# One-core adaLN block with gated linear attention and experts: four rotating PSUM banks with a table instead of two in turn

## The reference

```
h = layernorm(x) * (1 + ca) + sa
x = x + ga * attention(h)
h = layernorm(x) * (1 + cb) + sb
x = x + gb * (experts(h) + sigmoid(h @ sg) * shared(h))
```

```
o     = (Q e^G) @ S + tril(Qh @ Kh^T) @ V
S_new = S * e^glast + Ks^T @ V
out   = (o * rsqrt(mean(o*o) + eps) * norm_w * silu(h @ Wgate)) @ Wo
```

## Time and profile before

| | us |
|---|---|
| three runs | 458.25, 461.17, 461.62; median 461.17 |
| the profiled execution | 459.07 |
| its span | 457.3 |
| TensorE busy, mean granted clock | 401.1 (88%), 0.95 |
| VectorE, ScalarE, GpSimd busy | 238.7, 146.0, 147.7 |

### The profile page before, as it was taken

How to read it: one execution, slowest core, us unless ns; L and a number is a source line. 1 busy time by engine, 2 the same in 40 slices (tenths; PEclk the granted TensorE clock), 3 DMA queues, 4 the chain that set the end, 5 groups by cost and what they waited for, 6 DMA issues and landing times.

```text
span 457.3 us, 9813 instructions
## 1 busy us (share of the span) xinstructions
PE 401.1 (88%) x3848; PEld 245.4 (54%) x3849; DVE 238.7 (52%) x559; ACT 146.0 (32%) x295; POOL 147.7 (32%) x249
## 2 busy tenths in 40 slices
PE   3988889898989998998799999825999999999785
PEld 3434565575547575645544744612466666666353
DVE  3167556698588469221652552002255565565467
ACT  2566627444644422162022311000243333333000
POOL 8304104110510051020000057773017677677400
PEclk9999899998999799799899999975999999999899
DMA  8999000000000000084000012323023333321097
GB/s 262 296 309 240 3 5 1 3 3 4 0 3 4 1 1 4 2 268 114 0 0 0 2 47 106 107 106 106 0 83 105 89 122 97 84 92 47 32 313 238
DMA packets 31230, 37.72 MB, mean 82 GB/s; under 512 B 4176, under 2 KB 28115, under 8 KB 31189
## 3 DMA queue, kind: packets, MB, share of 16 engines
q1 hardware_dynamic: 27780, 28.63, 21.2%
q0 software_dynamic: 3408, 8.51, 5.3%
HBM read 21.15 MB, written 16.90 MB: 83 GB/s over the span
## 4 chain that ended last, share of the span: by engine, by line
PE 70%; DVE 8%; ACT 6%; another core or an unknown queue 6%; issue 4%; DMA 4%; SPq 1%; DVEq 0%; POOLq 0%; ACTq 0%
PE work L1295 13%; PE at_ps L1630 11%; PE work L1325 7%; PE work L1305 4%; PE work L1651 4%; PE work L1499 4%; PE at_ps L1360 3%; PE work L1653 3%; PE work L1445 3%; DMA arena<-ys_tokens 2%; PE at_ps L1348 2%; PE at_ps L1614 2%; PE work L1436 2%; PE o_even L1413 2%
## 5 line engine op out<-in xcount | busy, mean ns | idle before, releaser
L582 POOL DMA_INDIRECT ys_tokens<-er_pos,goal_u x39 | 43.8, 1123 | 44.3 <-DVE er_pos L1218 38.5
L1305 PE MATMUL work<-sdn_sb,hs 128*128 128x256 f32 x192 | 48.5, 396 | 8.9 <-issue 4.7
L1630 PE MATMUL at_ps<-arena 128*128 x156 | 54.5, 472 | 0.4 <-ACT arena L802 0.4
L553 POOL DMA_INDIRECT xs_sorted<-h2tok,pos_u x32 | 31.6, 987 | 72.0 <-DVE pos_u L910 62.6
L984 DVE TENSOR_TENSOR hs<-work,hs 128x512 f32<-128x512 f32 (+1 forms) x24 | 16.6, 692 | 63.8 <-PE work L1295 50.4
L598 ACT ACTIVATE hs<-work 128x512 f32<-128x512 f32 (+1 forms) x24 | 14.3, 596 | 103.1 <-PE work L1295 85.5
L1305 PEld LDWEIGHTS work<-sdn_sb,hs 128*128 128x128 f32 x192 | 34.0, 189 | 22.5 <-issue 12.4
L516 POOL TENSOR_TENSOR sq<-sq,sg 128x512 f32<-128x512 f32 x8 | 10.0, 1276 | 100.1 <-issue 100.1
L1295 PE MATMUL work<-h2T,sup_sb 128*128 128x512 f32 x80 | 37.9, 623 | 0.6 <-DVE hs L984 0.3
L1630 PEld LDWEIGHTS at_ps<-arena 128*128 128x128 f32 x156 | 26.5, 190 | 14.9 <-issue 6.6
L806 ACT ACTIVATE arena<-at_ps 128x176 f32<-128x176 f32 x39 | 12.4, 318 | 59.7 <-PE at_ps L1630 43.6
(11 more groups left out here) (225 smaller groups left out, 776.8 us busy)
## 6 DMA issues: line engine op xcount, KB each, us to landing
xs_sorted<-arena SPq DMA_DIRECT2D x10, 526.0 KB, 10.3
h2tok<-xs_sorted SPq DMA_DIRECT2D x20, 263.0 KB
arena<-ys_tokens SPq DMA_DIRECT2D x8, 512.0 KB, 7.3
arena<-in_e_up SPq DMA_DIRECT2D x8, 352.0 KB, 5.4
x_sb<-in_x SPq DMA_DIRECT2D x4, 512.0 KB, 7.4
out_rows<-x_sb SPq DMA_DIRECT2D x16, 128.0 KB, 4.8
sup_sb<-in_s_up SPq DMA_DIRECT2D x2, 640.0 KB, 4.7
hs<-in_wmod SPq DMA_DIRECT2D x1, 1024.0 KB, 8.2
```

What stands on the lines that cost most here:

```text
L553: g.indirect_dma_start(out=xs_dram, out_offset=bass.IndirectOffsetOnAxis(ap=pos_u[:, k, t:t + 1], axis=0), in_=h2tok[:, t, :], in_offset=N ...
L582: g.indirect_dma_start(out=ys_dram, out_offset=bass.IndirectOffsetOnAxis(ap=goal_u[:, i:i + 1], axis=0), in_=yout[:, q % 2, u, :], in_offs ...
L1305: ins = t_.matmul(o[:, t * HID:(t + 1) * HID], hs[0:m, f, tk], sdn_sb[0:m, f, :], start=(f == 0), stop=(f == FTS - 1))
L1630: ins = t_.matmul(at_ps[2 + u % 2][:, 0:2 * FE], xT[:, u % 2, k * P:(k + 1) * P], eup[:, bass.ds(e, 1), k, :].rearrange("p a n -> p (a n)" ...
```

## The change

The rotating ring gets four banks: `work[0]`, `work[1]`, `at_ps[2]`, `at_ps[3]`. For the products of slots 0 to 3 a fixed table says which bank each uses (`BANKS`); from slot 4 on, banks 0 and 1 are used in turn as before. `begin` waits for the last product in the same bank (`LAST_IN_BANK`), not for the product two places ahead. Z becomes a product of the ring, in banks 2 and 3. KV leaves the ring: its halves go to `at_ps[0]` and `at_ps[1]`, with a semaphore `kv_full` of their own. The modulation rows of the second batch row go to `o_ps`.

Four places in TensorE's order change. K half 0 moves up between HT and RT. The two halves of KV move up: half 0 stands behind WO half 0, half 1 behind LR. G half 1 is taken apart: the first halves of the scores' quarters (q = 0, 1) stand before its first matmul, the other two quarters between its two pairs. The waits for `kh_ready` and `qeo_ready` stand ahead of G half 0. On VectorE `next_state(s)` moves up, between `add_out(b, 0)` and `add_out(b, 1)` (in slot 0 between `finish_mod_rows(0)` and `scale_wo()`), and so ahead of `z_min(s + 1)`.

The core of the diff:

```diff
+BANKS = {("G", 0): 0, ("G", 1): 1, ("V", 0): 0, ("HT", 0): 1, ("HT", 1): 0, ("K", 0): 1, ("RT", 0): 0, ("K", 1): 2,
+         ("Q", 0): 3, ("Q", 1): 1, ("V", 1): 0, ("KT", 0): 2, ("KT", 1): 3, ("XT", 0): 1, ("XT", 1): 0, ("WO", 0): 2,
+         ("LR", 0): 3, ("WO", 1): 1, ("Z", 0): 2, ("Z", 1): 3}
...
+BANK_OF = dict(UNITS)
+LAST_IN_BANK = {key: next((k for k, w in reversed(UNITS[:n]) if w == at), None) for n, (key, at) in enumerate(UNITS)}
...
+                "Z": [(zabs_done, 2 * blk + j + 1), (zmin_done, 2 * blk + j + 1)],
...
         def bank(key):
-            return work[TURN[key] % 2]
+            return (work + at_ps[2:])[BANK_OF[key]]
...
                 if b >= 0:
                     gated_out(b)
-                    add_out(b)
+                    add_out(b, 0)
                 else:
                     finish_mod_rows(0)
+                if s < NBLK:
+                    next_state(s)
+                if b >= 0:
+                    add_out(b, 1)
+                else:
                     scale_wo()
                 if s + 1 < NBLK:
                     z_min(s + 1)
-                if s < NBLK:
-                    next_state(s)
...
             def begin(key):
-                n = TURN[key]
-                if n >= 2:
-                    for s, val in released(UNITS[n - 2]):
+                if LAST_IN_BANK[key]:
+                    for s, val in released(LAST_IN_BANK[key]):
                         pe.wait_ge(s, val)
...
-            def scores_first(b):
+            def scores_first(b, first_q, last_q):
-                for q in range(2 * KC):
+                for q in range(first_q, last_q):
                     for j in range(NPAIR):
+                        if q == 0 and j == 0:
+                            pe.wait_ge(kvin_ready, 2 * b + 2)
                         if q == 0 and j == KC:
-                            pe.wait_ge(zabs_done, 2 * b + 2)
-                            pe.wait_ge(zmin_done, 2 * b + 2)
+                            pe.wait_ge(zabs_done, 2 * min(b + 2, NBLK))
+                            pe.wait_ge(zmin_done, 2 * min(b + 2, NBLK))
...
-            def key_values(s):
-                pe.wait_ge(ktok_ready, 2 * s + 2)
-                pe.wait_ge(v_ready, 2 * s + 2)
...
+            def key_values(s, e):
+                if e == 0:
+                    pe.wait_ge(ktok_ready, 2 * s + 2)
+                    pe.wait_ge(v_ready, 2 * s + 2)
+                    if s == 0:
+                        pe.wait_ge(modr_ready, 2)
+                    else:
+                        pe.wait_ge(mln_done, 2 * s)
...
                     project(("G", s, 0), wgate_sb, 0, hT)
...
+                    if b >= 0:
+                        scores_first(b, 0, KC)
+                        project(("G", s, 1), wgate_sb, 1, hT, between=lambda: scores_first(b, KC, 2 * KC))
                     else:
-                        pe.wait_ge(modr_ready, 2 * BATCH)
-                    scores_first(b)
-                if s < NBLK:
-                    project(("G", s, 1), wgate_sb, 1, hT)
+                        project(("G", s, 1), wgate_sb, 1, hT)
...
+                    project(("K", s, 0), wk_sb, 0, hT)
+                if h >= 0:
...
                     router(h)
...
+                if s < NBLK:
+                    key_values(s, 0)
                 if s + 1 < NBLK:
                     low_rank(s + 1)
+                if s < NBLK:
+                    key_values(s, 1)
...
                 if s + 1 < NBLK:
                     gate_logits(s + 1)
-                if s < NBLK:
-                    key_values(s)
```

More of the change, by code:

```diff
@@ L55 @@
 SH_F = [(f * P, min(P, FS - f * P)) for f in range(FTS)]
+BANKS = {("G", 0): 0, ("G", 1): 1, ("V", 0): 0, ("HT", 0): 1, ("HT", 1): 0, ("K", 0): 1, ("RT", 0): 0, ("K", 1): 2,
+         ("Q", 0): 3, ("Q", 1): 1, ("V", 1): 0, ("KT", 0): 2, ("KT", 1): 3, ("XT", 0): 1, ("XT", 1): 0, ("WO", 0): 2,
+         ("LR", 0): 3, ("WO", 1): 1, ("Z", 0): 2, ("Z", 1): 3}
 def unit_order():
-    units = [("MODC", 0, 0)]
-    def both(kind, blk):
-        units.extend([(kind, blk, 0), (kind, blk, 1)])
-    def fill(s, place):
-        for part, blk, i in FILL.get((s, place), ()):
-            units.extend([("SD", blk, i)] if part == "D" else [("SA", blk, i)] + [("SB", blk, i)][:i < FTS - 1])
@@ L68, in unit_order, with put, turn, part @@
-    both("XT", 0)
-    units.append(("LR", 0, 0))
-    for s in range(NBLK + 1):
-        b, h = s - 1, s - 2
-        if s < NBLK:
-            both("G", s)
-        fill(s, "gates")
-        if s < NBLK:
-            units.append(("V", s, 0))
+    units = [(("MODC", 0, 0), 0)]
+    def put(kind, blk, j):
+        units.append(((kind, blk, j), BANKS[kind, j]))
+    def turn(*keys):
+        for key in keys:
+            units.append((key, 1 - units[-1][1] % 2))
+    def part(kind, blk, i):
+        turn(*([("SD", blk, i)] if kind == "D" else [("SA", blk, i)] + [("SB", blk, i)][:i < FTS - 1]))
@@ L77, in unit_order @@
+    def fill(s, place):
+        for kind, blk, i in FILL.get((s, place), ()):
+            part(kind, blk, i)
+    for kind, j in (("XT", 0), ("XT", 1), ("LR", 0), ("Z", 0), ("Z", 1)):
+        put(kind, 0, j)
+    for s in range(NBLK):
+        b, h = s - 1, s - 2
+        put("G", s, 0)
+        put("G", s, 1)
+        put("V", s, 0)
         if h >= 0:
-            both("HT", h)
+            put("HT", h, 0)
+            put("HT", h, 1)
+        put("K", s, 0)
         if h >= 0:
-            units.append(("RT", h, 0))
@@ L81, in unit_order @@
-        fill(s, "half")
-        fill(s, "second")
-        if s < NBLK:
-            both("K", s)
-        fill(s, "norm")
-        if s < NBLK:
-            both("Q", s)
-            units.append(("V", s, 1))
-            both("KT", s)
+            put("RT", h, 0)
+        for kind, j in (("K", 1), ("Q", 0), ("Q", 1), ("V", 1), ("KT", 0), ("KT", 1)):
+            put(kind, s, j)
         if s + 1 < NBLK:
-            both("XT", s + 1)
+            put("XT", s + 1, 0)
+            put("XT", s + 1, 1)
@@ L100, in unit_order @@
+    fill(NBLK, "half")
+    fill(NBLK, "second")
+    fill(NBLK, "norm")
+    turn(("WO", NBLK - 1, 0), ("WO", NBLK - 1, 1))
     fill(NBLK, "stats")
     fill(NBLK, "ln")
-    both("HT", NBLK - 1)
+    turn(("HT", NBLK - 1, 0), ("HT", NBLK - 1, 1))
     fill(NBLK, "transposed")
-    units.append(("RT", NBLK - 1, 0))
+    turn(("RT", NBLK - 1, 0))
     fill(NBLK, "top2")
@@ L107, in unit_order @@
     for f in range(EARLY_UP, FTS):
-        units.extend([("SA", NBLK - 1, f)] + [("SB", NBLK - 1, f)][:f < FTS - 1])
-    both("SD", NBLK - 1)
+        part("U", NBLK - 1, f)
+    turn(("SD", NBLK - 1, 0), ("SD", NBLK - 1, 1))
     return units
```

114 lines of the change are left out of this document (54 added, 60 removed).

## The result

| | before | changed |
|---|---|---|
| median of the runs, us | 461.08 (4 runs, 458.25 to 461.62) | 449.06 (4 runs, 445.96 to 450.14) |
| profiled execution, its span | 459.07, 457.3 | 445.96, 444.2 |
| granted clock, mean | 0.950 | 0.966 |
| first indirect DMA of the scatter, us | 267.14 | 254.97 |

The ratio is 0.9738 (95% interval 0.9684 to 0.9791). All ratios here leave out executions over 1.5% slower than the fastest one of the same kernel; the medians take all. The medians differ by 12.0 us, where 9.0 were forecast. The forecast was 452.1; the rival "the clock comes back everywhere" had 447.4. What was measured lies between them, nearer to the rival.

A forecast was written before the change was run, and what follows sets the result against it. Slots 0 to 3 were taken as bound by TensorE's own work plus short waits on a two-bank ring. 8.4 - 0.6 - 0.2 - 0.15 - 0.3 + 1.9, say 9.0, off 459.07, plus 2.1, gave 452.1 us; range 447.0 to 457.5.

The forecast's parts named there:

- the clock comes back everywhere: Rival: all 6.6 us lost to low clock in slots 1 to 3 return, not 1.9; 447.4 us, chance 0.20.
- G behind KV: Start of slots 1 to 3: G's waits for VectorE's read-out of KV all go, 3.4 us.
- KT; V half 1 of slot 0: KT's four waits for V's read-out go, 1.9 us; V half 1's wait for Q in slot 0 goes, 1.3.
- router of slots 2 and 3: K half 0 between HT and RT covers the two waits for HT's read-out, 1.5 us gained.
- WO: WO's waits for XT go, 0.3 us; in slot 3 WO half 0 comes 0.15 before KT half 0 is read.
- scores' wait for Z, and taking apart: First scores wait for Z's read-out, 0.2 us three times, 0.6 lost; cutting G half 1 and KV costs 0.3.
- XT in slot 2: XT waits for ScalarE's rows if K's read-out ends late; 0.2 us lost, bounds 0 and 1.0.
- holes for "issue": TensorE's holes called "issue", 5.2 us in this stretch, stay or land elsewhere: 0, bounds plus and minus 1.7 us.
- clock, slots 1 to 3: Of 6.6 us lost to low clock, 1.5 from the first fall and 0.4 of the rest return, 1.9.
- the waits change place: Rival: scores wait for Z, XT for its rows, the clock returns nothing; gain 4.0, 457.2 us, chance 0.15.
- Slower: Rival: openings of slots 1 to 3 lose 32-row overlap and the clock falls; 7 us slower, 468, chance 0.05.
- Swallowed later: Rival: longer "issue" holes or clock falls in slot 4 take the gain; 461 us, chance 0.08.

The follow-up runs named there:

- r3: Changed kernel with KV whole behind Z again and the next state behind Z's read-out on VectorE; 426.44 us, ratio 0.9687.
- r4: Changed kernel with all four moves of the order undone, only the four banks and their table kept; 430.28 us, ratio 0.9762.
- r2: Changed kernel with K half 0 put back behind the second share of the chunks; 433.33 us, ratio 0.9826.
- r5: Changed kernel with the scores whole ahead of G half 1 again; 432.78 us, ratio 0.9770.
- r6: Changed kernel with VectorE reading Z out ahead of the second addition to x; 433.98 us, ratio 0.9815.
- r8: Changed kernel with KV whole behind Z and the next state behind Z's read-out in slots 0 to 2, both early only in slot 3; 427.86 us, ratio 0.9696.
- r10: Changed kernel with the ten DMAs that zero the rows held until both halves of slot 0's KV are made; 442.76 us (one run).
- r9: r8 with the scores whole ahead of G half 1 as well; 428.00 us, ratio 0.9700.
- r12: The kernel of r3 once more, in more rounds; 430.37 us, ratio 0.9653.
- r7: Changed kernel with the router of slots 2 and 3 held by four more ScalarE copies of HT half 1; 439.67 us, ratio 0.9946.
- r11: The changed kernel once more, with no edit, as a further sample of its clock; 430.51 us, ratio 0.9777.
- r1: The changed kernel again, with no edit, on another chip as its yardstick; 430.32 us, ratio 0.9749.

## Why the prediction was right, point by point

| step | taken, us | measured, us |
|---|---|---|
| G behind KV | +3.4 | +3.4, but by the banks alone (r3, r4) |
| KT; V half 1 of slot 0 | +1.9; +1.3 | gone, both |
| router of slots 2 and 3 | +1.5 | gone; r2 brings back 1.6 |
| WO | +0.3 - 0.15 | -0.2 (0.3 before, 0.5 after) |
| scores' wait for Z, and taking apart | -0.6 - 0.3 | -3.7 |
| XT in slot 2 | -0.2 (to -1.0) | -1.2 |
| holes for "issue", the scores' apart | 0 | -0.2: KV's 0.6 became 2.0, the others fell from 2.7 to 1.5 |
| HT | not named | -0.3 (0.4 before, 0.7 after) |
| clock, slots 1 to 3 | +1.9 (to +6.6) | +6.6, 5.1 of it by K half 0 (r2, r4) |

By the measured sizes: 8.4 (with all of WO's 0.3) - 0.5 - 3.7 - 1.2 - 0.2 - 0.3 + 6.6 = 9.1. Another 0.5 is an earlier start of slot 0 (19.5 for 20.0). Slot 4 came 11.4 earlier; 1.8 of that has no row of its own.

Direction and mechanism of the waits were right: every wait that was to go went, at the forecast size, and the two that were to stay stayed. The sum was right partly by luck. The clock gave 4.7 more than taken, and the other rows 4.65 less (scores and taking apart 2.8, XT 1.0, WO 0.35, HT 0.3, "issue" 0.2): they cancel to a tenth. And by two of the prediction's own signs it was wrong: "The forecast is wrong if XT or the scores wait a microsecond or more", and XT waited 1.2 us and the scores 1.0 in slot 2; and the first scores were to take not clearly over 1.2 us in sum, where in slot 2 their three pieces take 1.94.

*"Of the other 5.0 I take 0.4, since small products still stand together there."* That is the term that was furthest off. The small products do still stand together; the clock stays up. The router of slots 2 and 3 (from 101 and 141 us in the changed kernel) was followed by full clock in every kernel with K half 0 ahead of the router and the router not held (the changed one three times, r3, r5, r6, r8 and r10, also r9 and r12, whose fall at 115 us lies behind XT) and by a fall in both slots in every kernel with a hole there (before, r2, r4, r7), 0.7 to 3.5 us behind the router's start. Slot 4's router keeps its wait of 0.7 us in every kernel, and there the clock fell 0.5 to 2.8 us behind its start in ten of the fourteen profiles (in the changed kernel at 175 us, behind 173.3) and was already low in three; in r3 it stayed up. The rival "the clock comes back everywhere" had this right and got 0.20. The rule quoted beside it, short idle times between groups that cycle through PSUM banks make the clock swing ("TensorE: Matmul & The Clock Gate" in the Trainium skill), is borne out here in its first part, with holes of 0.8 us. The cycling through banks is not what counts at the router: it waits for ScalarE's copy of HT, and in r4, with the waits for banks gone, both falls stayed.

*"Price 0 to 0.5 each; I take 0.2"* and *"I take 0.3, near the abutting rows."* Together 3.7. The first counted VectorE's instructions right and missed that GpSimd's product, moved to the same time, blocks one of them. It took the addition to x as ending at T + 0.9; it ended at T + 1.8, of which 0.74 is the block and 0.3 a scan that ended later than taken. The second was judged by rows in which G is followed by the scores once. A single split of the scores costs 0.3 to 0.4 us (r3, r4, r5), about what was taken in sum for all. The state early accounts for 2.1 of the 3.7: r3 gets them back.

*XT* lost 1.2 instead of 0.2. From the end of K's read-out to the end of ScalarE's rows there are 7.0 us (108.42 to 115.46), as computed, and TensorE needs 7.9 from K's end (106.4) to XT, for the 8.2 computed. But K's read-out ended 2.0 us behind K, where before it was 0.9 (113.1, 114.0) and the wait begins at 1.2. VectorE did not lose time, TensorE won it: from the start of slot 2 to K's end it needed 24.2 us before (88.9 to 113.1) and 23.4 now, since the router's waits and the low clock are gone. Waits that go and a clock that rises bring the next reader's deadline forward; the terms weren't independent. r2, r4 and r7, which have the router's holes and falls, don't wait at XT.

The rival "the waits change place" (0.15) was thus half true, 3.7 + 1.2 lost where it had 3.4 + 1.0; the clock, to which it gave nothing, made the difference. "Slower" asked for two falls and none came. "Swallowed later" neither: 11.4 at slot 4, 12.2 at the scatter, 13.1 in the span.

What stays open is slot 1. The clock fell between 40 and 75 us in r5, r6, r7, r9 and r10, in none of the three profiles of the changed kernel, nor in r2, r3, r4, r8 and r12. The falls before 50 us (r5, r6, r7) stand in or right behind KV's hole, in three of the seven profiles with a hole of 1.7 us or more and in none of the others of the new ring (0.8 at most); that is a link, not a proof, and r11 had the longest hole and no fall. The falls from 53 to 75 us (r5, r6, r9, r10) are not explained, but for r10's, which begins within a wait of 10.9 us: neither KV's hole nor the order of the scores does it (r9 has 0.5, r6 has the scores split, r4 has them whole and no fall).

## What to carry to other kernels

Price a removed wait at its own length, then look at whether the clock fell near it: here two holes of 0.8 us ahead of narrow products came with falls that cost 5.1 us, three times their length. Before work is moved earlier, test whether more banks alone free the waiting engine: they did, and the early state only put GpSimd's product beside VectorE's additions. The falls here cost 1.7 us each at the least and come in some executions of a kernel and not in others (r3 and r12 are one kernel), so two orders that differ by 3 us want the clock of each run beside its time, and a mark in the profile that ends with the stretch that was changed.

## What the runs showed of the hardware

*VectorE and GpSimd exclude each other for these products*: the fp32 addition 128x512 took 1.43 us beside GpSimd's L551 and 0.69 alone, as shown. The profile lists the blocked time as part of the instruction and not as a wait.

*Holes of 0.8 us can be enough for a fall, and 2.0 can be too little.* In slots 2 and 3 the clock fell behind the router's 0.8 us every time (six of six in before, r2 and r4); behind slot 4's 0.7 it did not in r3. XT's wait of 2.0 us was followed by none in r3 and r8 and by one in r9; with 1.7 it was in r12.

*The chips differ in the scatter, not in the changed stretch.* The profiles of the changed kernel on the first chip and on the second (r1) reach the scatter at 254.97 and 255.76 us and then part. TensorE behind it, first chip, then r1:

```profile
275.43 10.99 PE L1322 MATMUL work<-sdn_sb,hs 128*128 128x256 f32 x43 [1.41 <-DVE hs L999]
...
301.70 2.07 PE L1312 MATMUL work<-hT,sup_sb 128*128 128x512 f32 x2 [5.33 <-DVE tmp L1007]
```

```profile
276.21 12.00 PE L1322 MATMUL work<-sdn_sb,hs 128*128 128x256 f32 x48 [1.41 <-DVE hs L999]
288.14 14.00 PE L1312 MATMUL work<-hT,sup_sb 128*128 128x512 f32 x32
```

L1312 starts 13.6 us later on the first chip, behind five holes called "issue" (7.7 us) and this wait of VectorE; the spans differ by 15.2:

```profile
300.77 0.88 DVE L1007 SCALAR_TENSOR_TENSOR tmp<-work,sgate,rows 128x256 f32<-128x256 f32 x2 [25.40 <-remote]
```

Before had the same wait there (25.18 us), so it cancels in the comparison. Its cause was not tried.
